# A gated cross-attention layer with routed experts: expert tiles of two halves of 128 slots, the first bias folded into the product, and the first product two tiles ahead

## The reference, cut to what matters

```python
def _L0_ffn_ref(x, rW, rb, W1, b1, W2, b2, sW1, sb1, sW2, sb2):   # D 128, HIDDEN 512, 8 experts, top 2, 2 shared
    xf = x.reshape(-1, D)                                          # 4096 tokens
    sh = _gelu(jnp.einsum('td,sdh->sth', xf, sW1) + sb1[:, None, :])
    shared = (jnp.einsum('sth,shd->std', sh, sW2) + sb2[:, None, :]).mean(axis=0)
    gates = xf @ rW + rb
    topk_vals, topk_idx = jax.lax.top_k(gates, TOP_K)
    topk_probs = jax.nn.softmax(topk_vals, axis=-1)
    ...
    h = _gelu(jnp.einsum('td,edh->eth', xf, W1) + b1[:, None, :])
    y = jnp.einsum('eth,ehd->etd', h, W2) + b2[:, None, :]
    moe = jnp.einsum('te,etd->td', w, y)
    return (shared + moe).reshape(B, L, D)
x = x + jnp.tanh(g_xattn[0]) * _L0_xattn_ref(_layernorm(x), ctx_1024, ctx_1024, mask, ...)   # 32 x 128 tokens, 16 heads
x = x + jnp.tanh(g_ffn[0]) * _L0_ffn_ref(_layernorm(x), ...)
```

## Time and profile before

| what | value |
|---|---|
| median of 3 runs | 455.58 us (455.02 to 456.61) |
| the profiled execution: its time, its span | 454.94 us, 453.1 us |
| PE busy | 386.3 us, 85% of the span |
| DVE, ACT, POOL busy | 384.9, 340.8, 309.7 us |
| granted TensorE clock, mean | 0.977 |

### The profile page before, as it was taken

The page is one execution under the profiler, slowest core; times in us unless marked ns, Lnnn a source line. Parts: engine busy times, 40 slices in busy tenths (PEclk is TensorE's granted clock), DMA queues, the critical chain, the costliest instruction groups (busy, mean ns, idle before and its releaser), DMA issues.

```text
span 453.1 us, 14622 instructions
## 1 busy us (share of the span) xinstructions
PE 386.3 (85%) x5155; PEld 316.6 (70%) x5155; DVE 384.9 (85%) x947; ACT 340.8 (75%) x677; POOL 309.7 (68%) x431
## 2 busy tenths in 40 slices
PE   0558889997999899988789999998999999999910
PEld 0335677786788788766557776777899999999900
DVE  7696668978876987899778999887799999999986
ACT  0635677787888788878789986775888888888844
POOL 6252222799899899978777767774177777777740
PEclk9999999999999999999899999999999999999975
DMA  7968884354333334474221111112223333355229
GB/s 192 314 196 214 206 186 110 90 138 98 92 92 98 87 95 107 101 229 175 92 66 49 55 37 53 49 48 69 70 83 96 97 90 93 94 156 158 69 78 294
DMA packets 71686, 53.43 MB, mean 118 GB/s; under 512 B 7209, under 2 KB 63476, under 8 KB 71616
## 3 DMA queue, kind: packets, MB, share of 16 engines
q1 hardware_dynamic: 64896, 43.15, 35.9%
q0 software_dynamic: 4544, 8.44, 5.6%
q10 hardware_dynamic: 2176, 0.91, 0.8%
HBM read 29.51 MB, written 24.33 MB: 119 GB/s over the span
## 4 chain that ended last, share of the span: by engine, by line
POOL 23%; PE 21%; DVE 20%; issue 13%; DMA 10%; SPq 6%; ACT 4%; POOLq 0%; DVEq 0%; ACTq 0%
POOL yd L650 9%; DVE HH L1533 5%; PE pAtt L1144 4%; DMA scr<-QKS 4%; PE pAtt L1090 2%; PE pS L1132 2%; PE pE L1132 2%; DVE t_MX L1257 2%; POOL t_STG L558 2%; POOL t_W2l L562 2%; POOL QKS L548 2%; PE pAtt L928 1%; DMA t_STG<-in_W 1%; POOL xs L628 1%; POOL t_XF L572 1%
## 5 line engine op out<-in xcount | busy, mean ns | idle before, releaser
L650 POOL DMA_INDIRECT yd<-Y,XR x78 | 86.8, 1113 | 37.6 <-issue 23.2
L1257 DVE TENSOR_REDUCE t_MX<-pS 128x4 f32<-128x512 f32 x128 | 86.8, 682 | 22.6 <-PE pS L889 20.0
L748 ACT ACTIVATE PT<-pE,t_mbias,t_scl 128x512 f32<-128x512 f32 x128 | 96.9, 789 | 2.7 <-PE pE L889 2.7
L628 POOL DMA_INDIRECT xs<-t_STG,t_pos x64 | 66.2, 1034 | 23.1 <-issue 14.3
L1563 DVE SCALAR_TENSOR_TENSOR HR<-GG,t_sc,HR 128x512 f16<-128x512 f32 x78 | 58.6, 751 | 2.8
L1144 PE MATMUL pAtt<-t_W2h,HR 128*128 x624 | 59.2, 219 | 0.7 <-DVE HR L1563 0.7
L889 PE MATMUL pS<-t_K,t_Q 128*128 128x128 f16 x512 | 52.0, 228 | 8.5 <-DVE t_MX L1257 5.1
L1144 PE MATMUL pAtt<-t_W2l,HR 128*128 x312 | 54.4, 219 | 0.0
L828 ACT ACTIVATE GG<-pS,t_b1T,t_inv 128x256 f32<-128x256 f32 x78 | 39.8, 561 | 16.9 <-PE pS L1132 16.9
L889 PE MATMUL pE<-t_Q,t_K 128*128 128x128 f16 x512 | 49.9, 220 | 1.6 <-DMA t_Q<-MPl 0.6
L1144 PEld LDWEIGHTS pAtt<-t_W2h,HR 128*128 128x128 f16 x624 | 49.6, 98 | 1.1 <-issue 0.9
(11 more groups left out here) (280 smaller groups left out, 1042.7 us busy)
## 6 DMA issues: line engine op xcount, KB each, us to landing
xs<-t_padrow SPq DMA_DIRECT2D x10, 516.0 KB, 5.1
XR<-xs SPq DMA_DIRECT2D x39, 129.0 KB, 2.3
scr<-QKS SPq DMA_DIRECT2D x16, 256.0 KB, 2.4
t_Q<-scr SPq DMA_DIRECT2D x16, 256.0 KB
t_K<-scr SPq DMA_DIRECT2D x32, 128.0 KB
t_STG<-in_W SPq DMA_DIRECT2D x7, 512.0 KB, 6.6
YY<-yd SPq DMA_DIRECT2D x14, 256.0 KB, 4.2
t_X<-in_x SPq DMA_DIRECT2D x4, 512.0 KB, 7.7
```

What stands on the lines that cost most here:

```text
L628: g.indirect_dma_start(k.xs, bass.IndirectOffsetOnAxis(ap=pos[:, n:n + 1], axis=0), k.PAY[:, n, :], None).then_inc(h.di[q], 16)
L650: g.indirect_dma_start(k.yd, bass.IndirectOffsetOnAxis(ap=XR[u][:, q, D:ROW], axis=0), Y[u][:, q, :], None, bounds_check=2 * T - 1, oob_is ...
L748: act.activation(PT[:, m % NPT], pE[g % 2][:], ACT.Exp, bias=k.mbias[:, bt:bt + 1], scale=k.scl[:, bt:bt + 1]).then_inc(s.exp, 1)
L1257: v.tensor_reduce(out=MX[:, n // G % 2, n % G // 4, m % 2, m // 2::2], in_=pS[n % 2][:], axis=AX_X, op=ALU.max).then_inc(s.max, 1)
```

## The change

`TILE` becomes 128. `NTILE` = 71 tiles are worked through in `NDUO` = 36 pairs ("duos") of two tiles, each half with an expert of its own; the last duo has one half. Then:

- `routed_up` makes 24 matmuls of 128 columns for a duo instead of 12 of 256, each half with its own weights; it runs two duos ahead of `routed_down`, and chunks share PSUM banks in pairs.
- the routed gelus are two of 512 columns for a duo instead of four of 256, without a bias; half of the rounding moves from DVE to ACT (`routed_rounding`).
- `routed_result` is one instruction for each half.
- the tile numbers are read two at a time, 13 times in the shared stage, once after it, and then inside the routed loop on PE and DVE, until all 71 are there; ACT needs none any more.
- the first bias is folded in: the last feature is set to 1, the last row of W1, sW1 and rW is subtracted from the other rows (`fold_last_row` on POOL in turns 3 to 5, from broadcast copies of the last rows that SP reads in turns 1 to 3), and the biases take that row's place. The W2 reads move from turns 1 to 3 to turns 4 to 6, the bounds of W2 two turns later, and W2 is split behind all of W1.

```diff
-TILE = 256
+TILE = 128
+DUO = 2 * TILE
+NDUO = -(-NTILE // 2)
+LASTC = D - 1
...
-    FIRST_W2 = 12
+    FIRST_W2 = 2 * NE
...
-    LOADS = 3
+    LOADS = 2
...
+            def load_last_rows(n):
+                w = (io.W1, io.sW1)[2 * n >= E]
+                e = 2 * n % E
+                for j in range(2):
+                    sp.dma_start(k.weight_pieces[PIECES + n][:, j * HID:(j + 1) * HID], w[e + j, LASTC, :].partition_broadcast(P)).then_inc(k.s_row[n // 3], 16)
+            def hidden_biases():
+                sp.wait_ge(s.fold, PIECES)
+                sp.dma_start(k.STG[LASTC:D, 0:E * HID], io.b1.rearrange("(o e) h -> o (e h)", o=1)).then_inc(k.s_b1, 16)
+                sp.dma_start(k.STG[LASTC:D, E * HID:NE * HID], io.sb1.rearrange("(o e) h -> o (e h)", o=1)).then_inc(k.s_b1, 16)
...
-                for n in {1: range(4, 6), 2: range(6, 8), 3: range(8, 10)}.get(t, ()):
-                    load_weights(n)
+                if t == 1:
+                    load_weights(PIECES - 1)
+                for n in {1: (0,), 2: (1, 2), 3: (3, 4)}.get(t, ()):
+                    load_last_rows(n)
+                if t == LAG + 2:
+                    hidden_biases()
+                for n in {LAG + 1: (0, 1), LAG + 2: (2, 3), LAG + 3: (4,)}.get(t, ()):
+                    sp.wait_ge(s.fold, n + 1)
+                    load_weights(PIECES + n)
...
+            def fold_last_row(n):
+                if n == 0:
+                    g.wait_ge(s.sq, PIECES)
+                g.wait_ge(k.s_row[n // 3], 16 * 2 * (3, 2)[n // 3])
+                for j in range(2):
+                    piece = k.weight_pieces[n][:, j * HID:(j + 1) * HID]
+                    ins = g.tensor_tensor(piece, piece, k.weight_pieces[PIECES + n][:, j * HID:(j + 1) * HID], ALU.subtract)
+                ins.then_inc(s.fold, 1)
...
                 if t == SPLIT:
                     g.wait_ge(s.ws, 1)
+                    g.wait_ge(k.s_b1, 32)
                     tables()
+                for n in FOLDS.get(t, ()):
+                    fold_last_row(n)
...
-                act.activation(G32[i % 2][:, c, :], pU[c][:, 0:TILE], ACT.Gelu, bias=k.b1T[:, bass.ds(e * NC + c, 1)], scale=k.inv[:, 3:4]).then_inc(r.gelu, 1)
+                act.activation(G32[i % 2][:, ch, 0:wide], pair_of_chunks(i, half)[:, :, 0:wide], ACT.Gelu, scale=k.inv[:, 3:4]).then_inc(r.gelu, 1)
+            def routed_rounding(i):
+                wide = TILE * parts_of(i)
+                act.wait_ge(r.gelu, 2 * i + 2)
+                wait(act, r.dn, i - M + 1)
+                act.activation(HR[i % M][:, 0, 2:4, 0:wide], G32[i % 2][:, 2:4, 0:wide], ACT.Copy, scale=k.sc[:, 2:3]).then_inc(r.hia, 1)
...
+                last = parts_of(i) - 1
                 for c in range(NC):
-                    wait(pe, r.gelu, NC * (i - 1) + c + 1)
-                    for step, (w, part) in enumerate(((k.W1h, 0), (k.W1l, 0), (k.W1h, 1))):
-                        ins = pe.matmul(pU[c][:, 0:TILE], w[:, bass.ds(e * HID + c * P, P)], XE[i % M][:, part, :], start=(step == 0), stop=(step == 2))
-                    ins.then_inc(r.up, 1)
+                    if c % 2 == 0:
+                        wait(pe, r.gelu, 2 * (i - 2) + c // 2 + 1)
+                    out = pair_of_chunks(i, c // 2)[:, c % 2, :]
+                    for q in range(last + 1):
+                        tok = slice(q * TILE, (q + 1) * TILE)
+                        for step, (w, part) in enumerate(((k.W1h, 0), (k.W1l, 0), (k.W1h, 1))):
+                            ins = pe.matmul(out[:, tok], w[:, bass.ds(es[2 * i + q] * HID + c * P, P)], XE[i % M][:, part, tok],
...
-                            ins = pe.matmul(pA[i % 2][:, q, :], HR[i % M][:, part, c, q * P:(q + 1) * P], w[:, bass.ds(e * HID + c * P, P)],
+                            ins = pe.matmul(pA[i % 2][:, q, :], HR[i % M][:, part, c, q * P:(q + 1) * P], w[:, bass.ds(es[2 * i + q] * HID + c * P, P)],
...
-            for i in range(NTILE):
-                if i + 1 < NTILE:
-                    routed_up(i + 1, es[i + 1])
-                if i + 3 < NTILE:
+            routed_up(1)
+            for i in range(NDUO):
+                if i + 3 < NDUO:
                     row_transposes(i + 3)
-                routed_down(i, es[i])
+                tile_experts.load()
+                if i + 2 < NDUO:
+                    routed_up(i + 2)
+                routed_down(i)
...
-                    v.tensor_scalar(HR[i % M][:, 0, ch, :], G32[i % 2][:, ch, :], k.sc[:, 2:3], None, ALU.mult).then_inc(r.hi, 1)
+                    if half == 0:
+                        v.tensor_scalar(HR[i % M][:, 0, ch, 0:wide], G32[i % 2][:, ch, 0:wide], k.sc[:, 2:3], None, ALU.mult).then_inc(r.hi, 1)
+                    else:
+                        v.wait_ge(r.hia, i + 1)
...
+                for q in range(parts_of(i)):
+                    ins = v.scalar_tensor_tensor(out=Y[u][:, q, :], in0=pA[i % 2][:, q, :], scalar=k.down[:, 0:1], in1=k.b2[:, bass.ds(es[2 * i + q] * D, D)],
+                                                 op0=ALU.mult, op1=ALU.add)
...
+                tile_experts.load()
+                routed_result(i)
```

More of the change, by code:

```diff
@@ L241, in layer @@
     SPLIT = LAG + 3
-    FIRST_W2 = 12
-    SPLITS = [(which, e, half) for which, e in ((0, 8), (0, 9), (0, 0), (0, 4), (0, 1), (0, 5), (1, 0), (1, 1), (1, 2), (1, 3), (0, 2), (0, 6), (1, 4),
-                                                (0, 3), (0, 7), (1, 5), (1, 8), (1, 9), (1, 6), (1, 7)) for half in range(2)]
+    FIRST_W2 = 2 * NE
+    SPLITS = [(which, e, half) for which, e in ((0, 8), (0, 9), (0, 0), (0, 4), (0, 1), (0, 5), (0, 2), (0, 6), (0, 3), (0, 7),
+                                                (1, 0), (1, 1), (1, 2), (1, 3), (1, 4), (1, 5), (1, 8), (1, 9), (1, 6), (1, 7)) for half in range(2)]
     UNITS = len(SPLITS)
@@ L271, in layer @@
     SUNITS = 2 * NGR
-    FIRST_DONE = (T + E * (TILE - 1)) // TILE
-    assert FIRST_DONE + 2 * N <= NTILE
-    LOADS = 3
+    FIRST_DONE = -(-((T + E * (TILE - 1)) // TILE) // 2)
+    assert FIRST_DONE + 2 * N <= NDUO and SLOTS <= XS_ROWS
+    LOADS = 2
     LOADING = SUNITS - 7
@@ L367, in load_results, with parts_of @@
         eng.dma_start(YY[:, j, R * n:R * n + R, :], yv[:, j, R * n:R * n + R, :]).then_inc(f.ld[j][n], 16)
+    def parts_of(i):
+        return min(2, NTILE - 2 * i)
     def all_scattered(eng):
         for u in range(N):
-            eng.wait_ge(r.st[u], 32 * len(range(u, NTILE, N)))
+            eng.wait_ge(r.st[u], 16 * sum(parts_of(i) for i in range(u, NDUO, N)))
     class TileExperts:
@@ L801, in shared_body @@
                     wait(act, h.lo, NC * (i - 2) + c + 1)
-                    col = (E + i % 2) * NC + c
-                    act.activation(HS[i % 2][:, c, :], pU[c], ACT.Gelu, bias=k.b1T[:, col:col + 1], scale=k.inv[:, 3:4]).then_inc(h.gelu, 1)
+                    act.activation(HS[i % 2][:, c, :], pU[c], ACT.Gelu, scale=k.inv[:, 3:4]).then_inc(h.gelu, 1)
                     if c - 1 in on_scalar(i):
                         rounding(i, c - 1)
-                    if c % 2 and i >= LOADING:
-                        tile_experts.load()
                     if i == 3 and c == 0:
@@ L1229, in first_scales @@
                 link(v.tensor_scalar(root, root, 1.0, float(ROOT_ABOVE), ALU.mult, ALU.add))
+                v.scalar_tensor_tensor(out=k.tmp2[:, 0:1], in0=k.bound[:, 3:4], scalar=2.0, in1=k.bound[:, 2:3], op0=ALU.mult, op1=ALU.add)
                 link(v.scalar_tensor_tensor(out=k.bound[:, 2:3], in0=k.bound[:, 3:4], scalar=XN_NORM2, in1=k.bound[:, 2:3], op0=ALU.mult, op1=ALU.add))
+                link(v.tensor_copy(k.bound[:, 3:4], k.tmp2[:, 0:1]))
                 scales(v, link, k, 2, 5, 15)
@@ L1311, in choices @@
                     v.wait_ge(l.idx, TABLES)
-                link(v.tensor_tensor(k.G[:, rows, :], k.G[:, rows, :], over_n(k.rb), ALU.add))
                 for gates, top, one in ((k.G[:, rows, :], m1, O1), (G2[:], m2, O2)):
@@ L1625, in program @@
         k.s_c, k.s_x = ([outer.enter_context(nc.semaphore(f"{n}{c}")) for c in range(NT // CHUNK)] for n in ("c_ctx", "c_x"))
-        k.s_one, k.s_pad, k.s_padk, k.s_b2, k.s_rest = (outer.enter_context(nc.semaphore("c_" + n)) for n in ("one", "pad", "padk", "b2", "rest"))
+        k.s_one, k.s_pad, k.s_padk, k.s_b2, k.s_rest, k.s_b1 = (outer.enter_context(nc.semaphore("c_" + n)) for n in ("one", "pad", "padk", "b2", "rest", "b1"))
+        k.s_row = [outer.enter_context(nc.semaphore(f"w_row{n}")) for n in range(2)]
         k.keep = outer
```

137 lines of the change are left out of this document (74 added, 63 removed).

## The result

The changed kernel takes 509.66 us (median of 4 runs) against 455.69 us for the kernel before (4 runs): ratio 1.1173, 95% interval 1.1141 to 1.1206, slower. Its profiled execution took 509.87 us, with a span of 508.1 us and a mean granted clock of 0.976.

What follows compares the result with a forecast made beforehand. PE was taken as full before, its sequencer hidden; after the change the sequencer binds: 35.5 duos x 4.3 us + 17.4 us of reads = 170 us, so +55 us on 454.94 gives 510 us, range 486 to 528.

Steps and rivals of the forecast that it cites:

- What bounds before: Routed stage before: PE full at 2.87 us a tile, DVE and POOL close, PE's sequencer hidden at 2.4 us.
- Fewer slots, -10.0 us: Routed stage: 35.5 tiles of 256 in place of 39, at PE's 2.87 us, take off 10.0 us.
- Products of 128 columns, free: Routed products on PE: 24 first and 24 second at 56 ns and 4 transposes, 2.89 us a duo, as before.
- The rival in which weight loads set the pace: First products on PE: loads not overlapped make a duo 4.0 us and the kernel 481 us; chance 0.02.
- Addresses, 0.118 us each: PE's sequencer, routed stage: 32 address instructions a duo, 3.8 us, with three waits 4.3 us against 2.89 of matmul.
- The rival in which addresses are hidden: Routed stage: matmul stays the bound if an address holds products back under 0.075 us; 448 us; chance 0.08.
- Reads, 22 x 0.79 = 17.4 us, whole: PE's sequencer in the routed loop: 22 reads of two tile numbers, 0.79 us each, uncovered, add 17.4 us.
- the rival in which they are covered: Routed loop on PE: products already issued hide the reads of tile numbers; +38 us, 493 us; chance 0.12.
- The other engines fit: Routed stage: DVE, ACT and POOL stay under 4.3 us a duo; new order, shared banks and two-duo lead cost nothing.
- The folded bias and the front, 0 (-2 to +2): Ahead of the routed stage: POOL's subtractions, SP's row reads and the moved W2 reads cost 0, between -2 and +2 us.
- The sum: Routed stage: 35.5 x 4.3 + 17.4 = 170 us from 318.2; POOL done near 492.2, +55 us, 510 us.
- The clock, and costs above: Routed stage: clock falls to 1.2 GHz, 546 us, chance 0.02; dearer or remade addresses, waits, reads, about 532 us, chance 0.10.

Runs made afterwards that it cites:

- e13: The kernel before with its weight addresses packed (195 instructions instead of 624) and PE's tile numbers read three at a time inside second products; 455.80 us, ratio 1.0012.
- e10: The changed kernel with addresses packed (321 instructions instead of 1136) and asked for in separate places, the read moved into the middle of the second product; 450.01 us, ratio 0.9868.
- e6: The changed kernel with the old 39 tiles of 256 of one expert, 16 addresses a tile, all numbers read ahead; rest of the change kept; 459.66 us, ratio 1.0072.
- e3: The kernel before with each first product of 256 columns split into two of 128, same weights and address; 456.44 us, ratio 1.0030.
- e4: The kernel before with first products in halves of 128 columns, second halves with their own addresses, 24 a tile instead of 16; 471.72 us, ratio 1.0379.
- e2: The changed kernel without PE's 22 reads of tile numbers in the routed loop; a fixed expert is copied from a register instead; 496.44 us, ratio 1.0867.
- e14: As e12, but without the ten row loads of the bias fold; POOL's subtractions stay, each on the piece itself; 446.27 us, ratio 0.9809.
- e12: As e10, but the router's 128 rows come in one transfer, its last row is spread over 128 partitions, and the bias row goes last; 449.89 us, ratio 0.9890.
- e8: The changed kernel with addresses packed, in one burst behind the read ahead of the first product; 32 reads in the loop instead of 22; 469.31 us, ratio 1.0297.

## Why the prediction was right

The forecast was 510 us, slower; measured were 509.66. The mechanism held, and two of its terms were off in opposite directions.

- *What bounds before.* Right for the sequencer: it is hidden, and packing its addresses changes nothing (e13). PE is full, as the forecast said; POOL keeps the same pace, and no run tells the two apart.
- *Fewer slots, -10.0 us.* Right in size: e10 against e6 is (1.0072 - 0.9868) x 455.7 = 9.3 us, some 1.5 us either way. The forecast took it from PE's tiles; POOL's scatters fall with them from 78 to 71, and the runs do not divide the gain between the two.
- *Products of 128 columns, free.* Right (e3). The rival in which weight loads set the pace is out.
- *Addresses, 0.118 us each.* Right: 0.12 us from e4 and the change's late period, and from the spacing of its weight loads. 4.3 us a duo was forecast, 4.27 measured, and early in the stage a matmul share of 60% by the count. With the addresses packed and spread the time falls by (1.1173 - 0.9868) x 455.7 = 59.5 us. The rival in which addresses are hidden is true only as far as 16 a tile, as before; at 24 (e4) they already show.
- *Reads, 22 x 0.79 = 17.4 us, whole.* They stand whole on the path, and the rival in which they are covered is out (e2). The size was too large: the 0.79 us was that of a read of three numbers, and a read of two lasts 537 ns instead of 794. So the early period is 4.90 us and not 5.1. The two periods and e2's trace give 0.63 us, 22 x 0.63 = 13.9 us; e2's median gives 0.75 us.
- *The other engines fit.* Right in the change: their waits end at PE. That the lead of two duos costs nothing holds for the pace; in e6's trace it delays the first scatter by 2 us, which the forecast named in one of its rivals only.
- *The folded bias and the front, 0 (-2 to +2).* Wrong in size, beyond its own bounds: the first address came at 322.4 us instead of 318.2, and in e6's trace at 321.3. I had priced POOL's subtractions and the bytes of the row loads, which at equal bytes in turns 1 to 3 I took to be neutral. I had not looked at the small transfers of the router's rows, nor at what W2's reads in turns 4 to 6 and the rows ahead of them do to attention's loads. The runs name the row loads (e14, by intervals that nearly touch); the stall behind the 127 rows is seen in the trace and gone in e12, but no median shows its 3 us, and no run takes W2's late reads away.
- *The sum.* From 322.4 the stage took 164.4 us, against 170 forecast from 318.2. So 5.6 us too much in the stage and 4.2 too little ahead of it nearly cancelled: POOL was done at 491.8 us where 492.2 was forecast. The agreement to 0.3 us in the total is luck; the terms were good to some 4 us each.
- *The clock, and costs above.* The granted clock stayed full in the stage, and no address had to be made anew (1136 is 71 x 16).

By the ratios, the change is +59.5 us of addresses and reads, -9.3 us of slots and +3.3 us of front and lead. The three add up to the measured difference because they are steps from one run to the next (the change to e10, e10 to e6, e6 to before).

## What to carry to other kernels

When a tile gets smaller, ask what is paid per tile and not per element. Here two addresses that held an expert's number served three first products of 256 columns or six second ones of 128, and came to serve three of 128, and PE's sequencer, which no busy share counts, became the bound. Ask for such addresses side by side and not one before each product, and keep each stretch of sequencer work shorter than what the engine still has in hand; then the change that cost 12% gains 1.3% (e10). Beside PE, POOL's scatters then follow each other without a wait for a result, and ACT is busy for 64.58 of 70 us. A matmul engine's pace is read from the count of matmuls, not from its busy time.

## What the runs showed of the hardware that was not expected

- An instruction that packs up to six register operations lasts 74 ns (e8, median) where one of three lasts 46 and a single one 32; 320 of them in place of 1136 are enough to hide the addresses. The time goes far more by instructions than by operations.
- PE's sequencer runs ahead of the matmuls only so far: a read and six packed instructions in a row left PE dry for 0.47 us a duo although the sequencer's work of a whole duo was shorter than its products (e8); the same work in three places left no gap (e10).
- A DMA of 127 rows, issued in 0.24 to 0.37 us, was followed by a stall of 2.2 to 4.9 us on whichever transfer came next; behind 128 rows the next one was issued in 0.55 us (e12). That the number of rows is the reason is inferred, as e12 changed other transfers too.
